# Statistics, norms and the first quantisation of a two-layer kernel as steps per token tile on VectorE

## The reference

```python
x = x + L0_xattn(layernorm(x), ctx)   # causal self-attention plus cross-attention, 16 heads of 16
x = x + L0_ffn(layernorm(x))          # two linears on rounded values, a scale for each token
x = x + L1_xattn(layernorm(x), ctx)   # cross-attention
x = x + L1_ffn(layernorm(x))          # two linears on rounded values, one scale for the whole tensor

def rmsnorm(x):
    return x * rsqrt(mean(x * x, axis=-1) + 1e-5)
def act_quant(x):                      # L0_ffn, ahead of each linear
    scale = 127.0 / clip(max(abs(x), axis=-1), 1e-5)
    return clip(round(x * scale), -128, 127) / scale
```

## Time and profile before

| | us |
|---|---|
| median of 3 runs | 1926.49 |
| lowest and highest | 1925.32, 1931.07 |
| the profiled execution | 1921.53 |
| its span | 1919.7 |
| PE busy | 1685.9 (88%) |
| DVE busy | 1370.9 (71%) |
| ACT busy | 1156.6 (60%) |
| POOL busy | 659.1 (34%) |

### The profile page before, as it was taken

How to read it: one execution, slowest core, us unless ns; L and a number is a source line. 1 busy time by engine, 2 the same in 40 slices (tenths; PEclk the granted TensorE clock), 3 DMA queues, 4 the chain that set the end, 5 groups by cost and what they waited for, 6 DMA issues and landing times.

```text
span 1919.7 us, 29141 instructions
## 1 busy us (share of the span) xinstructions
PE 1685.9 (88%) x10052; PEld 732.4 (38%) x10064; DVE 1370.9 (71%) x2549; ACT 1156.6 (60%) x2178; POOL 659.1 (34%) x915
## 2 busy tenths in 40 slices
PE   4898889997999899998999899998999899678677
PEld 1344334423543344333542344333542354241236
DVE  6667767777687767777777758876777768638376
ACT  1374475566755585657655675567556676552597
POOL 3332523541454134522355044522354041140040
PEclk7898999999999999999999999999999999796998
DMA  7334313332242323331332324231333223014023
GB/s 198 88 104 127 89 34 95 83 93 69 60 110 63 85 67 93 84 97 56 94 87 73 86 56 115 75 90 56 95 84 86 59 56 96 0 52 147 23 88 111
DMA packets 106947, 159.49 MB, mean 83 GB/s; under 512 B 20656, under 2 KB 83248, under 8 KB 106800
## 3 DMA queue, kind: packets, MB, share of 16 engines
q1 hardware_dynamic: 101904, 156.43, 29.5%
q10 hardware_dynamic: 4896, 1.18, 0.3%
HBM read 105.00 MB, written 51.38 MB: 81 GB/s over the span
## 4 chain that ended last, share of the span: by engine, by line
PE 54%; DVE 25%; ACT 10%; POOL 4%; issue 4%; DMA 1%; ACTq 0%; SPq 0%; DVEq 0%; POOLq 0%
DVE nmax L1222 13%; PE acc L1459 13%; PE mx L1424 11%; PE st L1445 9%; PE misc L1399 6%; PE misc L1371 4%; PE misc L1486 3%; PE misc L1411 3%; ACT probs L965 3%; ACT tail_h L1035 2%; DVE hid L1176 2%; ACT tail_h L1020 1%; ACT hid L1000 1%; PE misc L1513 1%; ACT hqT L924 1%
## 5 line engine op out<-in xcount | busy, mean ns | idle before, releaser
L1222 DVE TENSOR_REDUCE nmax<-mx 128x1 f32<-128x512 f32 (+2 forms) x1376 | 872.2, 673 | 318.4 <-PE mx L1424 189.5
L965 ACT ACTIVATE probs<-st 128x512 f32<-128x512 f32 (+3 forms) x1536 | 764.2, 549 | 410.4 <-PE st L1445 261.4
L1424 PE MATMUL mx<-stack 96*128 96x512 bf16 (+3 forms) x1536 | 550.8, 371 | 124.0 <-DVE nmax L1222 100.0
L1445 PE MATMUL st<-stack 99*128 99x512 bf16 (+3 forms) x1536 | 542.7, 366 | 28.8 <-ACT probs L965 27.3
L1424 PEld LDWEIGHTS mx<-stack 96*128 96x128 bf16 x1536 | 151.5, 99 | 355.1 <-DVE nmax L1222 281.3
L1445 PEld LDWEIGHTS st<-stack 99*128 99x128 bf16 x1536 | 149.6, 99 | 355.6 <-ACT probs L965 196.5
L844 POOL TENSOR_TENSOR parts<-qk,zero 128x512 bf16<-128x512 f32 x78 | 81.2, 1041 | 211.7 <-ACT qk L948 211.7
L1459 PE MATMUL acc<-probs,v_x 128*32 128x512 f32 x1024 | 145.9, 644 | 0.0
L1459 PE MATMUL acc<-probs,v_f 128*32 128x512 f32 x1024 | 140.0, 619 | 0.4 <-ACT probs L965 0.3
L856 POOL TENSOR_TENSOR nparts<-nmax,zero 128x16 bf16<-128x16 f32 x96 | 21.3, 222 | 287.0 <-DVE nmax L1222 287.0
L1448 PE MATMUL st<-mask_st,identb 128*128 128x128 bf16 x512 | 111.7, 221 | 0.0
(11 more groups left out here) (248 smaller groups left out, 2096.1 us busy)
## 6 DMA issues: line engine op xcount, KB each, us to landing
parts_xk<-parts SPq DMA_DIRECT2D x48, 128.0 KB
parts_xq<-parts SPq DMA_DIRECT2D x48, 128.0 KB
stack<-parts_xq SPq DMA_DIRECT2D x32, 192.0 KB, 3.2
stack<-parts_xk SPq DMA_DIRECT2D x32, 192.0 KB, 3.7
parts_sk<-parts SPq DMA_DIRECT2D x48, 128.0 KB
parts_sq<-parts SPq DMA_DIRECT2D x48, 128.0 KB
stack<-parts_sq SPq DMA_DIRECT2D x32, 192.0 KB, 2.9
stack<-parts_sk SPq DMA_DIRECT2D x32, 192.0 KB, 3.4
```

Source lines behind the costliest of these rows:

```text
L965: act.activation(probs[:, j % P_SLOTS, c, T - w:], st_bank(n, 4 * j + c)[:, 0:w], ACT.Exp, scale=SCALE).then_inc(exp_done, 1)
L1222: dve.tensor_reduce(nmax[:, ring, first:first + NT * (len(cs) - 1) + 1:NT], src, AX.X, ALU.max, negate=True).then_inc(mx_free, 1)
L1424: last = pe.matmul(o, stack[0:ROWS, r, 0, c, P * i:P * i + P], stack[0:ROWS, r, 1, c, 0:w], start=True, stop=not causal)
L1445: last = pe.matmul(o[:, 0:w], stack[0:AUG, r, 1, c, P * j:P * j + P], stack[0:AUG, r, 0, c, T - w:T], start=True, stop=not causal)
```

## The change

Each of the blocks becomes a row of steps: `stats` five steps (the first tile's statistics; three times the next tile's statistics with the aggregate of the tile before; the last aggregate), `norm` four, `x_scale` two (the maximum, the token scales), `quant_x` five. The operations and their number stay as they were. What waits at the head of a block is waited for by its first step. GpSimd's part of `stats` stays at the last step, and its bias row at the last step of `norm`. The lists given to `deal` and `blend` are longer by these steps.

```diff
+def stats(b, k):
+    return [("stats", b, k, t) for t in range(NT + 1)]
+
+
+def norm(b, k):
+    return [("norm", b, k, t) for t in range(NT)]
+
 def tokens0(b):
-    return [("ctx_T", b, "A"), ("stats", b, "A"), None, None, ("norm", b, "A"), None, ("norm_T", b, "A"), None]
+    return [("ctx_T", b, "A")] + stats(b, "A") + [None, None] + norm(b, "A") + [None, ("norm_T", b, "A"), None]
...
 def ffn_norm(b):
-    return [("stats", b, "F"), None, None, None, ("norm", b, "F"), ("x_scale", b), ("quant_x", b), None, None, None, None,
-            ("quant_T", b), None, None]
+    return stats(b, "F") + [None, None, None] + norm(b, "F") + [("x_scale", b, 0), ("x_scale", b, 1)] + [("quant_x", b, t) for t in range(NT + 1)] + \
+        [None, None, ("quant_T", b), None, None]
...
 def layer1_last(b):
-    return [("stats", b, "E"), None, None, ("norm", b, "E"), ("finish", b), None, None]
+    return stats(b, "E") + [None, None] + norm(b, "E") + [("finish", b), None, None]
...
             def norm(s):
-                k = s.args[0]
-                if k in "FC":
+                k, t = s.args
+                if k in "FC" and t == NT - 1:
...
             def x_scale(s):
                 n = s.b.times(SCALARS)
-                dve.wait_ge(xn_done["F"], s.b.times(4, 4).at())
-                dve.tensor_reduce(tok["xmax"][:, :], xn_of(s, "F")[:, :, :], AX.X, ALU.max, apply_absolute_value=True).then_inc(scalars, 1)
+                if s.args[0] == 0:
+                    dve.wait_ge(xn_done["F"], s.b.times(4, 4).at())
+                    dve.tensor_reduce(tok["xmax"][:, :], xn_of(s, "F")[:, :, :], AX.X, ALU.max,
+                                      apply_absolute_value=True).then_inc(scalars, 1)
+                    return
```

More of the change, by code:

```diff
@@ L225, in layer1_norm @@
 def layer1_norm(b):
-    return [("stats", b, "C"), None, ("ctx_T", b, "C"), None, None, ("norm", b, "C"), None, ("norm_T", b, "C"), None]
+    return stats(b, "C") + [("ctx_T", b, "C"), None, None] + norm(b, "C") + [None, ("norm_T", b, "C"), None]
 def layer1_start(b):
@@ L799, in stats_ @@
             def stats_(s):
-                k = s.args[0]
+                k, t = s.args
+                if t < NT:
+                    return
                 per = 6 if k == "F" else 2
@@ L1114, in stats_, with stats_ready @@
             def stats_(s):
-                k = s.args[0]
+                k, t = s.args
+                if t == 0:
+                    stats_ready(s, k)
+                if t < NT:
+                    dve.bn_stats(stats[k][:, t, :], source(s, k)[:, t, :]).then_inc(stats_done[k], 1)
+                if t:
+                    dve.wait_ge(stats_done[k], s.b.times(4, t).at())
+                    wait_alone(dve)
+                    dve.bn_aggr(mv[k][:, t - 1, :], stats[k][:, t - 1, :]).then_inc(mv_done[k], 1)
+            def stats_ready(s, k):
                 if k == "A":
@@ L1125, in stats_, with norm_ready @@
                         wait_misc_read(dve, s, h, ("residual", s.key[1], "C"))
[L1126 to L1131, removed]
-            def norm(s):
-                k = s.args[0]
+            def norm(s):
+                k, t = s.args
+                if t == 0:
+                    norm_ready(s, k)
+                dve.tensor_scalar(xn_of(s, k)[:, t, :], source(s, k)[:, t, :], mv[k][:, t, 0:1], rstd[k][:, t:t + 1],
+                                  ALU.subtract, ALU.mult).then_inc(xn_done[k], 1)
+            def norm_ready(s, k):
                 dve.wait_ge(rstd_done[k], s.b.times(6 if k == "F" else 2, 2).at())
@@ L1137, in norm @@
                     dve.wait_ge(stored, s.b.times(32, 32).at())
-                for t in range(NT):
-                    dve.tensor_scalar(xn_of(s, k)[:, t, :], source(s, k)[:, t, :], mv[k][:, t, 0:1], rstd[k][:, t:t + 1],
-                                      ALU.subtract, ALU.mult).then_inc(xn_done[k], 1)
             def token_scales(n, peak_, r, am, inv, scale, mult, w, first):
@@ L1162, in quant_x @@
             def quant_x(s):
-                n = s.b.times(5)
-                dve.wait_ge(scalars, s.b.times(SCALARS, 6).at())
-                for t in range(NT):
+                n, t = s.b.times(5), s.args[0]
+                if t == 0:
+                    dve.wait_ge(scalars, s.b.times(SCALARS, 6).at())
+                if t < NT:
                     dve.tensor_scalar(xn_of(s, "F")[:, t, :], xn_of(s, "F")[:, t, :], tok["xq"][:, t:t + 1], MAGIC, ALU.mult,
                                       ALU.add).then_inc(quant, 1)
+                    return
                 dve.wait_ge(quant, n.at(NT))
```

## The result

| | before | after |
|---|---|---|
| median, us | 1925.9 (4 runs) | 1942.18 (4 runs, 1941.33 to 1942.87) |
| ratio | | 1.008, 95% interval 1.0061 to 1.0099 |
| span of the profiled execution, us | 1919.7 | 1939.5 |
| mean granted clock | 0.946 | 0.944 |

The changed kernel is slower by 16 us at the median and by 19.8 us between the two profiled spans. The forecast of 1934.5 had the sign and the main mechanism; it lies 8 us too low. The page of after shows that no engine has more to do worth speaking of. DVE's busy time rose by 5.9 us and PE's by 9.1, and the weight loads for maxima wait for DVE as long as before (277.3 us, 281.3 in the earlier trace rows). What is new in the waits is the last line: PE waits for GpSimd's split of the negated maxima. Before, that was 1.0 us in 6 waits.

The account below looks back on a forecast made before the run. PE, busy 88%, sets the pace, and DVE where PE waits for maxima. Terms: f1 to f3 +22.8, x0 and x1 -11.4, turns 1 and 7 -6, splits +2.4; about +8 on 1926.5 gives 1934.5 us, range 1907 to 1948.

Parts of the forecast that it names:

- The meeting: In f2, DVE's token scales run into GpSimd's bias row and last 2.7 us, not 0.9; PE idles nearly 3 us.
- The 0.6 us that the last norm tile would lose to GpSimd's split: In f2 at (2, 0), tile 3 costs its 0.41 us plus 0.6 for meeting GpSimd's split; 1.0 taken.
- The clock is at full speed in f2: Sign against the forecast, which expected a low clock in f2, adding 0.9 us for one values step there.
- The rival with the missed bias row: Token scales in f2 find GpSimd idle and take 0.9 us, clock stays: 1908 us, faster; chance 0.28.
- 1.1 for the steps: In f3, quantisation tile 3 at (1, 0) and the last step together cost 1.1 us, bounds 0.8 to 2.0.
- statistics behind a first maximum cost in full: In f1, two statistics steps at (1, 0) and (2, 0), about 0.45 us each, delay PE by 1.0 us together.
- another sign named against the forecast: Steps at (1, 0) and (2, 0) leaving no wait on PE would show the forecast wrong.
- The three idle terms: DVE's idle time in x0 and x1: 4.0 us behind gelu, 3.7 in x0's front, 0.3 in x1; 8.4 used.
- clock falls over x0 and x1: Rival: PE thin in x0 and x1 brings the low clock, 2 us a turn, 12 in all: 1946.5 us; chance 0.15.
- moves 2.9 us of PE from one unit to the next and costs nothing: Norm_T and v of C move one or two places later, past the end of x3, at no cost.
- the 0.4 of the sum: In s0, DVE's own split may wait for GpSimd's later k-projection splits: 0.4 us a turn, 2.4 in all.
- the stretches that were given nothing: Ahead of the first turn and behind the last, nothing is beside the steps and operations keep their order: no cost.

## Why the prediction was partly right

**f2: right.** The meeting was placed at T + 7.8, with T the projection's start on PE, and the bias row at T + 7.4. Measured from T = 827.88: the bias row at T + 7.4, the token scales at T + 7.4 too. The operation took 2.31 us and PE idled 2.96, "nearly 3 us" in the forecast. The 0.6 us that the last norm tile would lose to GpSimd's split were 0.5 (0.91 for 0.41 us). f2 came out at 19.3 against 20.2 us, since the clock fell later than assumed. "The clock is at full speed in f2" was one of the signs that the prediction named against itself, and with 0.99 in turns 1 to 5 that sign came: the low clock is there, but a unit later. That the meeting decides the sign is shown by moving one operation: 1942 to 1912 us. The rival with the missed bias row gave 1908 us, but its total is near for errors that offset each other: f1 to f3 gave 6.4 us and not 1, x0 and x1 16.7 and not 11.4, and x2 to s0, which it left out, lost 11.8. The meeting itself hung on little: DVE arrived 0.05 us behind the bias row's start and not 0.4, so that it happened is partly luck.

**f3: the mechanism was right, the size was not.** The forecast was 17.9, measured 19.5 us. The low clock came here whole (0.83) and costs 3.0 us, by the run with the late bias row, where the sum had put 0.9 us of it into f2 and 1.0 into f3. Without it f3 takes 16.4 us, 0.6 over the 15.8 before, where the sum had 1.1 for the steps; in these 0.6 stands GpSimd's late split of the maxima, 1.20 us of waiting, which the sum did not have. With the projections behind `negmax` that wait goes and f3 is 1.7 us shorter, which then reappear in part in f1 and x0+x1.

**f1: near the number by luck.** Forecast 17.6, measured 17.4 us. But f1 took 17.04 us before, by its matmuls, so the loss is 0.3 us a turn and not the 1.0 of the sum. The step "statistics behind a first maximum cost in full" failed: moved behind the second, they cost the same, and PE's matmuls in f1 have no wait for DVE over 0.2 us, which was another sign named against the forecast. (Behind (2, 0) of f2 the wait is there: 0.82 us after the last norm tile.) The one wait that is new in f1 is 0.53 us for GpSimd's split of the maxima.

**x0 and x1: the mechanism was right, the gain was mis-sized**, -18.6 for -11.4 us. The sum reckoned with DVE's idle time over both units, and x1 bears it out: DVE is busy for 18.97 of its 19.18 us, 0.2 idle where 0.3 were expected. The rest is arithmetic and base. The three idle terms, 4.0 behind `gelu`, 3.7 in front and 0.3 in x1, add up to 8.0 and not to the 8.4 of the prediction, which is 2.4 us over six turns. Turn 3, from which it started, took 48.3 us, while the six turns took 48.6 on average: 1.7 us. And x0's idle time came out at 7.3 us for 7.7. The clock of x1, 0.81 before, is 0.99 in the changed kernel, but there DVE and not PE sets the pace. The rival "clock falls over x0 and x1" was wrong in its sign. Where E stays in blocks and the maxima are spread, x1 of turn 3 is at 0.84 (21.04 and 21.80 us in the two runs that have it).

**x2, x3 and s0: the step that failed.** The prediction said "moves 2.9 us of PE from one unit to the next and costs nothing" and gave DVE's split 0.4 us a turn. The zone lost 2.3 us in turns 2 to 6 and 1.4 in turn 7, 13.0 in all. Between x3 and s0 the work moved about as forecast: PE's busy time fell by 2.3 us in x3 and rose by some 2.5 in s0. In length x3 gave 2.3 us and s0 took 3.0, since DVE's split lost 0.84 us to GpSimd's and PE waited 0.74 us more behind it, for the 0.4 of the sum. The step that failed is "costs nothing" for the other shifted steps: x2, which has no term in the sum, lost 1.6 us, 0.9 of it at a lower clock, and `hid_scale` is a step that moved into it. Putting the steps back to their places took the loss away. This term alone, 10.6 us too small, is more than the 8 us between forecast and median.

**Turns 1 and 7.** In turn 1, x1 and x2 together took 3.6 us less (51.3 to 47.7), where the forecast had 3. But s0 took 2.2 more: PE waited 0.97 us for norm C's last tile, a wait that is new, and 1.0 us more behind DVE's split, which took 1.41 us in this turn before and after. And x0 took 1.6 more, with a clock of 0.92 for 1.00. Turn 7's f1 won 3.8 us and f2 lost 2.0: -1.8 for -3. That `gelu` came later there is the likely cause of f2's loss, and not shown by itself.

**The sum.** Two terms erred by some 7 and 11 us in opposite directions. What remains of the 12 us between the forecast difference and that of the spans is spread: 3 us in turn 1, 3 in the stretches that were given nothing, 1 each in turn 7 and in f1 to f3.

Left open: what decides in which unit the clock falls. f3 took 16.4 us in some turns and 18.0 us in others of one execution, with the same order of instructions; and in the kernel before, f2 of turn 2 had a clock of 1.00 (18.65 us) behind the same stall of 2.3 us that has 0.91 behind it in the other turns.

## What to carry to other kernels

Before a block is parted or a list grows, look at what every other step does that is shifted with it, and on which in-order engine. Here the shifted steps (one bias row on GpSimd, one split, one token scale) cost more than the parted ones gained. Where two engines share work on the same memory, place the long operation of the one where the other has no short ones: this single move turned a loss of 16 us into a gain of 14 us. But look at the place to which it goes: among blocks the same move met another operation of DVE and cost some 11 us. The best version keeps the parted norms A, F and E, adds the bias row later, leaves x2 to s0 as they were and puts F's steps behind the second maximum: 1899 us, ratio 0.9869 (0.9842 to 0.9897). With the projections behind `negmax` as well it is the same.

## What the hardware showed

An operation of 128 x 4 elements can last as long as GpSimd's operation on 128 x 1024 beside it: 2.31 us for 0.14 us when GpSimd was idle, in the same kernel but for that. Larger ones end a little behind GpSimd's operation: a norm tile 0.15 us behind it (0.91 for 0.41 us), DVE's split 0.55 us behind it (1.53 for 0.69 us). GpSimd loses in the same way when it comes second: 0.67 for 0.21 us in f3. The Trainium skill, page "SBUF — State Buffer", section "SBUF: two separate sides", describes this as an exclusive lock held for the whole instruction, and these rows agree. The section ties it to VectorE operations in a two-port mode or with two inputs in SBUF. In the run with blocks and the late bias row (830.63 to 832.98 us), DVE's reciprocal and multiplication on data in PSUM ran beside it at their usual 0.26 and 0.42 us:

```profile
831.99 0.26 DVE L1260 RECIPROCAL rsum<-misc 128x16 f32<-128x16 f32 x1 [0.16 <-PE misc L1400]
832.28 0.42 DVE L1266 TENSOR_TENSOR xn_C<-misc,rsum 128x256 f32<-128x256 f32 x1
832.62 1.30 DVE L1194 TENSOR_SCALAR xn_F<-xn_F,tok_xq 128x256 f32<-128x256 f32 x4
```

The third line is the quantisation of four tiles in SBUF, begun 0.36 us before the bias row ended. It took 1.30 us where it took 1.13 in the kernel before. All of the difference is in the first tile, the longest of these four (ns, shortest, median and longest):

```profile
L1194 DVE TENSOR_SCALAR xn_F<-xn_F,tok_xq x4: 341/344/508, 832.6 to 833.6; 128x256 f32<-128x256 f32 x4
```

It ended 0.15 us behind the bias row, as the norm tile did behind its split, and as the first tile of turn 4 in the same run did behind the bias row of 1043.06. So an operation that meets GpSimd's shortly before its end loses little.
